# The down product of the last feed-forward, from float32 to three float32r products, in a four-layer gated cross-attention kernel

## The reference, cut to what matters

```
logits = x_flat @ router_w.T
probs = jax.nn.softmax(logits, axis=-1)
top_v, top_i = jax.lax.top_k(probs, K)            # K = 2, E = 8
top_v = top_v / jnp.sum(top_v, axis=-1, keepdims=True)
...
h = jax.nn.gelu(jnp.einsum('ech,ehf->ecf', expert_in, w1), approximate=False)   # h 256 -> f 1024
y = jnp.einsum('ecf,efh->ech', h, w2)                                            # f 1024 -> h 256
...
out = out + tok * (gate * keep.astype(x.dtype))[:, None]
```

## Time and profile before

| what | value |
|---|---|
| median of 3 runs | 1944.79 us (1943.92 to 1948.82) |
| the profiled execution's own time | 1942.3 us |
| its span in the trace | 1940.6 us |
| busy in the span: PE, PEld, DVE, ACT, POOL | 82%, 62%, 57%, 42%, 15% |
| the last feed-forward's tiles | from about 1643 us to the end |

### The profile page before, as it was taken

One profiled execution on the slowest core, in us unless ns is written; L12 is line 12 of the kernel. 1 busy time (PEld: TensorE's weight loads), 2 busy tenths in 40 slices (PEclk: granted clock), 3 DMA queues, 4 the chain that ended last, 5 costly groups with the idle time before them and its releaser, 6 DMA issues.

```text
span 1940.6 us, 29271 instructions
## 1 busy us (share of the span) xinstructions
PE 1598.8 (82%) x10374; PEld 1211.8 (62%) x10375; DVE 1104.1 (57%) x2555; ACT 817.6 (42%) x1817; POOL 300.2 (15%) x367
## 2 busy tenths in 40 slices
PE   5899883893888873578887999999969973999997
PEld 3566662782555542445554678788845552999997
DVE  5666628314899998766653454536459966222221
ACT  2455530323776742245554522213259951222221
POOL 2101100541121100111110000000111202333332
PEclk7899975897799987689988999999979985999999
DMA  7355234226554411534525000000266716422221
GB/s 162 53 81 78 45 121 178 44 36 123 113 115 95 84 55 46 77 51 69 70 34 219 24 1 1 1 0 1 58 88 103 123 63 231 152 38 38 33 37 28
DMA packets 86262, 144.10 MB, mean 74 GB/s; under 512 B 14032, under 2 KB 69768, under 8 KB 82938
## 3 DMA queue, kind: packets, MB, share of 16 engines
q1 hardware_dynamic: 66121, 102.76, 22.7%
q0 software_dynamic: 20016, 39.71, 12.8%
HBM read 75.50 MB, written 27.66 MB: 53 GB/s over the span
## 4 chain that ended last, share of the span: by engine, by line
PE 57%; DVE 24%; issue 6%; DMA 6%; ACT 4%; SPq 1%; POOL 0%; POOLq 0%; DVEq 0%; ACTq 0%
PE ps L1390 12%; PE ps L1498 7%; PE ps L1509 7%; PE ps L1359 4%; DMA Qpack<-QP 3%; DVE probs L2261 3%; PE ps L1030 3%; PE ps L886 2%; PE ps L977 2%; PE ps L1271 2%; PE ps L968 2%; PE ps L1280 2%; DVE hpart L2242 2%; PE ps L916 2%; PE ps L866 2%
## 5 line engine op out<-in xcount | busy, mean ns | idle before, releaser
L348 POOL DMA_DIRECT2D Kpack<-KP x192 | 101.1, 534 | 960.5 <-PE ps L1390 385.0
L1636 ACT ACTIVATE pT<-ps 128x512 f32<-128x512 f32 x256 | 151.7, 606 | 193.6 <-PE ps L971 100.0
L968 PE MATMUL ps<-Qpack,Kpack 99*128 99x256 bf16 (+1 forms) x768 | 167.6, 285 | 19.2 <-DMA Qpack<-MR 7.2
L1498 PEld LDWEIGHTS ps<-xgT,XNT 128*128 128x128 f32 x1248 | 147.7, 195 | 1.9
L1498 PE MATMUL ps<-xgT,XNT 128*128 128x128 f32 x1248 | 147.8, 278 | 0.0
L937 PE MATMUL ps<-Kpack,Qpack 97*128 97x256 bf16 x512 | 107.4, 298 | 42.1 <-DMA Qpack<-QP 19.0
L1509 PE MATMUL ps<-w,mid 128*128 x624 | 141.0, 379 | 0.0
L1918 ACT ACTIVATE mid<-ps 128x512 f32<-128x512 f32 x78 | 42.3, 595 | 202.9 <-PE ps L1498 202.9
L2162 DVE CUSTOM_DVE_ANT_0 Vb<-ps,mask_bf 128x256 bf16<-128x256 f32 x256 | 95.2, 419 | 55.2 <-PE ps L937 54.9
L1641 ACT ACTIVATE pT<-ps,nmax 128x256 f32<-128x256 f32 x256 | 120.4, 531 | 13.9 <-DVE nmax L2174 13.5
L1509 PEld LDWEIGHTS ps<-w,mid 128*128 128x128 f32 x624 | 115.6, 190 | 14.1
(11 more groups left out here) (318 smaller groups left out, 3265.3 us busy)
## 6 DMA issues: line engine op xcount, KB each, us to landing
Kpack<-KP POOLq DMA_DIRECT2D x192, 128.0 KB, 5.0
Qpack<-QP SPq DMA_DIRECT2D x192, 128.0 KB, 6.9
w<-in_w SPq DMA_DIRECT2D x16, 1024.0 KB, 6.3
ctxT<-in_ctxT SPq DMA_DIRECT2D x32, 256.0 KB, 7.8
h_rows<-in_h SPq DMA_DIRECT2D x16, 512.0 KB, 7.3
h<-h_rows SPq DMA_DIRECT2D x2, 4096.0 KB, 22.0
wd<-in_wd SPq DMA_DIRECT2D x4, 1536.0 KB, 14.3
xn_rows<-xn SPq DMA_DIRECT2D x16, 256.0 KB, 2.5
```

What stands on the lines that cost most here:

```text
L348: eng.dma_start(Kpack[j][DH * k:DH * (k + 1)].rearrange("d (e f) t -> d e (f t)", f=HALF), KP[par][:, part]).then_inc(done, 16)
L968: mm = pe.matmul(A[h % ring][:, t], Kpack[par][0:rows, h, t * P:(t + 1) * P], Qpack[par][0:rows, h], start=True, stop=L != 0)
L1498: mm = pe.matmul(bank[:, f % 4 * P:(f % 4 + 1) * P], w1_tile[k % 2][:, c, f * P:(f + 1) * P], xgT3[k % 2][:, c], start=c == 0, stop=c == K ...
L1636: act.activation(pT[h % 8][:], A[h % 2][:], ACT.Exp).then_inc(s["exp_done"], 1)
```

## The change

In `ffn3` alone, the down product is no longer made in float32. Both operands are written as a high part, rounded to float32r, and a low part, the rest, and for each of the 8 pieces PE makes three float32r products: high by high, high by low, low by high. For this:

- ACT, in `hidden`, makes the Gelu of each half twice, once to `mid3` in float32 and once to `mh3` in float32r (four instructions of 128 x 512 in place of two). DVE subtracts, `mid3` - `mh3`, in place, to `ml3` (`low_mid`, one instruction of 128 x 1024).
- The expert's w2 is split for each tile: ACT copies it in four pieces of 128 x 512 to `w2h_3` in float32r (`high_w2`), DVE subtracts each piece to `w2l_3` (`low_w2`). Both first read the expert's number into a register, which PE no longer does. `w2h_3` and `w2l_3` are single; they lie where X was. A piece may be overwritten when the down product of the tile before has used it (`f3_piece`, four counts a tile).
- The orders become, on ACT: hidden(t), high_w2(t), copy_w1(t+2); on DVE: copy_w1(t+2), low_mid(t), weigh(t-1), low_w2(t), copy(t+2). PE's order stays; down waits once for `ml3` and four times for a piece of `w2l_3`.
- Some semaphores of the two expert layers are merged under one name, with the counts shifted by a constant. ACT waits once, before its first Gelu, until X has been sent to DRAM; POOL waits for the same before its first gather.

```diff
@@ sbuf
-        X = sb("X", [P, NT, D], F32)
+        x_ctx = ExitStack()
+        X = sb("X", [P, NT, D], F32, x_ctx)
+        x_ctx.close()
+        X_r = sb("X_r", [P, NT, D], F32R)
...
-        mid3 = [sb(f"mid3_{i}", [P, HT, P], F32, f3c) for i in range(2)]
+        m3c = ExitStack()
+        mid3 = [sb(f"mid3_{i}", [P, HT, P], F32, m3c) for i in range(2)]
+        m3c.close()
+        ml3 = [sb(f"ml3_{i}", [P, HT, P], F32R, f3c) for i in range(2)]
         yg3 = [sb(f"yg3_{i}", [P, D], F32, f3c) for i in range(2)]
+        mh3 = [sb(f"mh3_{i}", [P, HT, P], F32R, f3c) for i in range(2)]
+        w2h_3, w2l_3 = (X_r[:, 8 * i:8 * i + 8] for i in range(2))
@@ tensor
                 def down(b, k):
                     t = GBUF * b + k
-                    e = expert(t)
-                    pe.wait_ge(s["f3_loaded"], e + 1)
-                    pe.wait_ge(s["f3_mid"], t + 1)
+                    pe.wait_ge(s["f3_ml"], t + 1)
                     wait(pe, s["f3_yg"], t - 1)
                     for c in range(HT):
-                        mm = pe.matmul(ps[5 + 2 * (k % 2)][:, 0], mid3[k % 2][:, c], w2_3[:, ds(e, 1), c].squeeze(1), start=c == 0, stop=c == HT - 1)
-                    mm.then_inc(s["f3_down"], 1)
+                        if c % 2 == 0:
+                            pe.wait_ge(s["f3_w2l"], W2_PIECES * t + c // 2 + 1)
+                        for j, (m, w) in enumerate(((mh3, w2h_3), (mh3, w2l_3), (ml3, w2h_3))):
+                            mm = pe.matmul(ps[5 + 2 * (k % 2)][:, 0], m[k % 2][:, c], w[:, c], start=c + j == 0, stop=c == HT - 1 and j == 2)
+                        if c % 2 == 1:
+                            mm.then_inc(s["f3_piece"], 1)
@@ scalar
                 def hidden(t, k):
                     act.wait_ge(s["f3_up"], t + 1)
-                    wait(act, s["f3_down"], t - 1)
+                    wait(act, s["f3_piece"], W2_PIECES * (t - 1))
                     for half in range(2):
-                        e = act.activation(mid3[k][:, 4 * half:4 * half + 4], UP3[k][half][:].rearrange("p a (c t) -> p (a c) t", t=P), ACT.Gelu)
+                        up = UP3[k][half][:].rearrange("p a (c t) -> p (a c) t", t=P)
+                        act.activation(mid3[k][:, 4 * half:4 * half + 4], up, ACT.Gelu)
+                        e = act.activation(mh3[k][:, 4 * half:4 * half + 4], up, ACT.Gelu)
                     e.then_inc(s["f3_mid"], 1)
+
+                def high_w2(t):
+                    e = act.value_load(expert3_i[0:1, ds(t, 1)], min_val=0, max_val=E3 - 1)
+                    act.wait_ge(s["f3_loaded"], e + 1)
+                    for p in range(W2_PIECES):
+                        wait(act, s["f3_piece"], W2_PIECES * (t - 1) + p + 1 if not isinstance(t, int) or t else 0)
+                        act.activation(w2h_3[:, 2 * p:2 * p + 2], w2_3[:, ds(e, 1), 2 * p:2 * p + 2].squeeze(1), ACT.Copy).then_inc(s["f3_w2h"], 1)
@@ vector
                 def weigh(t, k):
-                    dve.wait_ge(s["f3_down"], t + 1)
+                    dve.wait_ge(s["f3_piece"], W2_PIECES * (t + 1))
...
+                def low_mid(t, k):
+                    dve.wait_ge(s["f3_mid"], t + 1)
+                    dve.tensor_tensor(ml3[k][:], mid3[k][:], mh3[k][:], ALU.subtract).then_inc(s["f3_ml"], 1)
+
+                def low_w2(t):
+                    e = dve.value_load(expert3_i[0:1, ds(t, 1)], min_val=0, max_val=E3 - 1)
+                    for p in range(W2_PIECES):
+                        dve.wait_ge(s["f3_w2h"], W2_PIECES * t + p + 1)
+                        dve.tensor_tensor(w2l_3[:, 2 * p:2 * p + 2], w2_3[:, ds(e, 1), 2 * p:2 * p + 2].squeeze(1), w2h_3[:, 2 * p:2 * p + 2],
+                                          ALU.subtract).then_inc(s["f3_w2l"], 1)
+
                 def tile(t, k):
-                    if not isinstance(t, int) or t + 2 < RUN3:
+                    more = not isinstance(t, int) or t + 2 < RUN3
+                    if more:
                         copy_w1(t + 2, k)
+                    low_mid(t, k)
+                    if not isinstance(t, int) or t:
+                        weigh(t - 1, 1 - k)
+                    low_w2(t)
+                    if more:
                         copy(t + 2, k)
-                    weigh(t, k)
```

More of the change, by code:

```diff
@@ L77 @@
 PAIRS = NT // ST
+W2_PIECES = 4
 FREE = 1
@@ L316, in program @@
                  "experts_w0 experts_w1 experts_w2 experts_w3 experts_w4 experts_w5 experts_w6 experts_w7 "
-                 "f0_router f0_step f0_hot f0_list f0_idstep f0_idx "
+                 "router f0_step hot list f0_idstep f0_idx "
                  "f0_xt f0_xgT f0_up f0_mid f0_down f0_yg f0_scatter "
@@ L429, in low @@
             return x.bitcast(U16).rearrange("p (n two) -> p n two", two=2)[:, :, 0]
+        listed = E0 * (("ffn", 0) in stages)
         gathered = 16 * SL0 * (E0 // GBUF) * (("ffn", 0) in stages)
@@ L582, in ffn @@
                 if L == 0:
-                    sp.dma_start(wr0[:], a["wr0"]).then_inc(s["f0_router"], 16)
-                    sp.dma_start(br0[:], a["br0"].partition_broadcast(P)).then_inc(s["f0_router"], 16)
-                    sp.dma_start(bu0[:], a["bu0"]).then_inc(s["f0_router"], 16)
+                    sp.dma_start(wr0[:], a["wr0"]).then_inc(s["router"], 16)
+                    sp.dma_start(br0[:], a["br0"].partition_broadcast(P)).then_inc(s["router"], 16)
+                    sp.dma_start(bu0[:], a["bu0"]).then_inc(s["router"], 16)
                     send_rows(n, B - 1)
@@ L605, in ffn @@
                 else:
-                    sp.dma_start(wr3[:], a["wr3"]).then_inc(s["f3_router"], 16)
+                    sp.dma_start(wr3[:], a["wr3"]).then_inc(s["router"], 16)
                     for b in range(B - 2, B):
@@ L843, in layernorm @@
                     if pair == 1:
-                        pe.wait_ge(s[f"f{L}_router"], 48 if L == 0 else 16)
+                        pe.wait_ge(s["router"], 48 if L == 0 else 16 + 48 * (("ffn", 0) in stages))
                     if pair > 1:
@@ L1249, in lists @@
                 def lists(e):
-                    pe.wait_ge(s["f0_hot"], e + 1)
+                    pe.wait_ge(s["hot"], e + 1)
                     for t in range(NT):
@@ L1254, in lists @@
                                        lists0[:, e, t].rearrange("p v h -> p (v h)"), start=t == 0, stop=t == NT - 1)
-                    mm.then_inc(s["f0_list"], 1)
+                    mm.then_inc(s["list"], 1)
                 def turn(e):
@@ L1468, in ffn3 @@
                 for j in range(PAIRS3):
-                    pe.wait_ge(s["f3_hot"], j + 1)
+                    pe.wait_ge(s["hot"], listed + j + 1)
                     for t in range(NT):
@@ L1473, in ffn3 @@
                                        start=j + t == 0, stop=j == PAIRS3 - 1 and t == NT - 1)
-                mm.then_inc(s["f3_list"], 1)
+                mm.then_inc(s["list"], 1)
                 pe.wait_ge(s["f3_idx"], 1)
-                def expert(t):
-                    return pe.value_load(expert3_i[0:1, ds(t, 1)], min_val=0, max_val=E3 - 1)
                 def turn(b, k):
@@ L1928, in ffn3 @@
                         hidden(2 * i + k, k)
+                        high_w2(2 * i + k)
                         copy_w1(2 * i + k + 2, k)
@@ L1931, in ffn3 @@
                     hidden(t, t % 2)
+                    high_w2(t)
                     if t + 2 < RUN3:
@@ L2454, in softmax_rows @@
                 if L == 0:
-                    dve.wait_ge(s["f0_router"], 48)
+                    dve.wait_ge(s["router"], 48)
                     link(5 * r + 1, r, dve.tensor_tensor(route[2][:], logits, bc_exp(br0[:]), ALU.add))
@@ L2565, in hot @@
                     dve.tensor_tensor(hot0[e % 2][:], place0[:, :, e].unsqueeze(2).to_broadcast([P, NT, P]),
-                                      col[:].unsqueeze(1).to_broadcast([P, NT, P]), ALU.is_equal).then_inc(s["f0_hot"], 1)
+                                      col[:].unsqueeze(1).to_broadcast([P, NT, P]), ALU.is_equal).then_inc(s["hot"], 1)
                 def index(e):
-                    dve.wait_ge(s["f0_list"], e + 1)
+                    dve.wait_ge(s["list"], e + 1)
                     got = ps[3 + e % 2][:, 0, 0:5 * SL0].rearrange("p (v h) -> p v h", v=5)
@@ L2804, in route3 @@
                 chain(dve.tensor_scalar(expert3_i[:], expert3[:], E3 - 1.0, None, ALU.min))
-                dve.wait_ge(s["f3_list"], 1)
+                dve.wait_ge(s["list"], listed + 1)
                 got = ps[3][:].rearrange("p a b -> p (a b)")[:, 0:6 * TILES3].rearrange("p (v i) -> p v i", v=6)
@@ L2853, in ffn3 @@
                     tile(t, t % 2)
+                weigh(RUN3 - 1, (RUN3 - 1) % 2)
             for n, (kind, L) in enumerate(stages):
```

8 lines of the change are left out of this document (5 added, 3 removed).

## The result

| | before | after |
|---|---|---|
| median us (lowest to highest), 4 runs each | 1945.56 (1943.92 to 1948.82) | 1927.09 (1925.28 to 1929.23) |
| profiled execution, its span | 1942.3, 1940.6 | 1928.7, 1927.0 |

The ratio is 0.991, with a 95% interval of 0.9884 to 0.9936: 18.5 us faster by the medians, where 22 were forecast. The profile has only 13.6 us less. So there are two questions: whether the tiles got what the prediction gave them, and where some 4 to 8 us went.

What follows compares the result with a forecast made beforehand. PE was taken to bound the steady tiles at 7.25 us each; downs 1 to 36 save 0.61 us each, 22 in all, from the median 1944.8 to a forecast of 1923 us, own range 1917 to 1930.

Steps and rivals of the forecast that it cites:

- PE's part: Down on PE: 24 float32r products at 0.119 us, 2.85 in place of 3.46 us; period 7.25 to 6.64 us.
- The weight loads: Rival on PE: 24 weight loads at 0.190 us set the pace, 4.56 us a down, 42 us slower, 1987; chance 0.02.
- ACT's part: ACT's Gelus, four w2 copies (2.66 us) and w1 copy end at U + 5.82, 0.8 us less than the period.
- DVE's part: DVE's work with the new subtractions is 5.71 us a tile plus register-load gaps; it fits with little to spare.
- The first rival's case: Another engine sets the pace: DVE with both register gaps open, 7.07 us, 1938; or ACT at 7.2, 1943; chance 0.18.
- a sign of being wrong: The prediction is wrong if a register load keeps its gap behind queued work, or an ACT copy costs over 0.87 us.
- POOL: POOL's scatter and gather, held up to 0.7 us each by DVE's subtractions, total 4.3 of 6.64 us; nothing taken.
- Start: At the first tile, down(0) moves from ending at 1658.5 to starting at 1658.3 us's older schedule: gains 0.2 us.
- End: At the last tiles, down(38) waits for its subtractions; nothing gained or lost, the two end downs give nothing.
- The sum: Downs 1 to 36 save 0.61 us each, 22.0; the first 0.2, the rest nothing; forecast 1923 us.
- The range: Whole kernel: own range 1917 (product at 0.112 us) to 1930 (0.2 us a tile lost to waits).

Runs made afterwards that it cites:

- float32 run: Changed kernel, but PE makes down as 8 float32 products of the high parts, the low parts made but unused: 1946.39 us, period 7.25 us.
- run with one product: Changed kernel, but of PE's three down products only high by high is made, 8 in place of 24: 1882.78 us.
- both: Changed kernel with POOL's gather of tile t + 4 before scatter t and ACT's wait for X before its first w1 copies: 1921.70 us, ratio 0.9884.
- before, load at the gate: Kernel before the change, with the load of the last expert's weights held until the first tile's gate was applied: 1935.92 us.
- changed, again: The changed kernel without edits, run and profiled a second time: 1924.75 us, ratio 0.9903.
- last load just ahead: Changed kernel, with the load of the last expert's weights held until the first tile's gate was applied: 1927.94 us.
- table early: Changed kernel, with ACT's wait for X in DRAM before its first w1 copies, not before its first Gelu: 1924.67 us.

## Why the prediction was right, point by point

- **PE's part: right.** 24 x 0.119 = 2.85 us was forecast, 2.86 measured; a gain of 0.61 us a tile, 0.60 measured; a period of 6.64, 6.65 measured. The pace of the same form in another stage could be carried over. The float32 run shows that nothing else took part in it.
- **The weight loads: the rival is wrong.** PEld is busy for all of the 212.69 us, and the pace is 0.119. The Trainium skill's rule (Perfetto Trace Analysis, Identifying the Most-Contended Engine) takes this busy share, beside the share of peak FLOP/s, for the measure of headroom; here it left 6% before the change, and half as many loads again went with less time.
- **ACT's part: mis-sized, on the safe side.** Forecast was a wait of 0.8 us for up in each tile, it is 1.6. The term is 4 x 0.665 for the w2 copies: they last 0.65 each but start 0.52 apart, 2.21 us in all. That is 0.45 of the difference of 0.8; most of the rest is the same overlap between the Gelus, the copies and the w1 copy.
- **DVE's part: right in kind, mis-sized.** Four subtractions take 2.5 us and not 2.76, for the same reason (0.60 apart). The second register load leaves 0.42 us, forecast 0.25. That DVE "fits with little to spare" was too dark: the run with one product shows 1.1 us to spare. The first rival's case, a cycle near PE's with gaps of 0.7 us on both loads, does not occur: they are 0.58 and 0.42 us in the changed kernel. But the prediction's reason against it, that loads are covered when DVE is late, holds only in part. In the run with one product one load in two kept a gap of 0.5 to 1.0 us. This was named as a sign of being wrong; it did no harm because PE's period is 1.1 us longer.
- **POOL: the step that failed.** "the rows are gathered four tiles ahead, so I take nothing." The step weighed POOL's busy time, but not that its gather stands behind a scatter that waits for a gate which the change moves one step later, nor that the early gathers run while 2 MB loads are under way. It cost 3.67 us in the profiled execution, 1.5 of them by the clock that fell behind the gap, 1.9 in the second, and none in the runs in which the load came later. The hold by DVE's subtractions that the step did weigh, up to 0.7 us, did not come: the scatter takes 1.60 us. (The instruction that held the gather of the earlier trace rows is not the one shown beside it, which began while the gather was already held, but the one before, from 336.68 to 338.97 us.)
- **Start: a term left out.** Down(0) was to gain 0.2 us and lost 1.3. The table load, 1.28 us, stands in none of its terms: a second wait in front of the first Gelu put it on the path. With ACT's wait moved up ("both") down(0) ends 3.63 us behind the first up products, 0.04 sooner than before.
- **End: right.** From the start of the last up product to the end it is 21.3 us before (1940.6 less 1919.3) and 21.2 after (1927.0 less 1905.8).
- **The sum.** 22 forecast. In the profile 36 x 0.598 = 21.5, less 3.67 at tile 4, less 1.3 at down(0), less 0.6 ahead of the first up product (the product that begins the stage ran at a granted clock of 0.62, before at 0.69), and 1.4 more by the clock of the first up products: 17.3, and the stages differ by 17.4. In the second profile, whose clock is that of the kernel before, 21.5 less 1.9 less 1.3 are 18.3, and the stages differ by 18.4. The medians differ by 18.5.
- **The range.** 1927.1 lies in it by its upper end, which was set for 0.2 us a tile lost to waits. Nothing was lost so; what took its place were two losses that the prediction did not have. The tiles were right by their mechanism, the closeness of the rest was in part luck.

## What to carry to other kernels

When PE sets the pace, take the pace of the new product form from a stage that has it, and then lay the other engines' new work out in time over one period. Take instructions of one kind at the distance of their starts. Then follow what a moved instruction releases on a queue that the change does not touch: here a gate one step later held a scatter, and the gather behind it on POOL. A prefetch should not stand behind a wait for a result. It is the first tiles, while large loads still run, in which this shows. And where a product behind a gap is long, look at the granted clock before looking for a wait.

## What the runs showed of the hardware

- A gather of 128 KB that was issued 0.3, 0.5 and 1.9 us behind a 2 MB load landed after 7.5, 8.2 and 7.9 us (the last by the transposes' start); the median was 2.8 us. Issued 0.5 us ahead of the load in the kernel before it landed after 5.5 us, 0.8 ahead ("before, load at the gate") after 4.9, and neither was late.
- Behind a gap of 1.94 us in PE's work (changed, profiled) and one of 2.35 (one product) the granted clock fell to the lower level for 3.4 us. It stayed at 1.00 behind gaps of 1.65, 1.31 and 0.80 us ("changed, again", "last load just ahead", "float32 down"). The gap alone does not tell: with one product the clock also fell at 1659.0 us, behind a gap of 1.66 and a down(0) that kept waiting for its pieces.
- POOL's scatter took 1.62 us on average before and 1.60 after the change, but 2.27 us in the run with one product. What decides is what runs when it starts. Between 1680 and 1860 us of the changed kernel 26 of 27 scatters start just ahead of DVE's subtractions and last 1.6 us, though these run beside them for 1.6 us; the one that starts under a subtraction takes 2.05. With one product all 33 start under one and last 1.6 to 3.6 us. The Trainium skill (SBUF — State Buffer, Who interferes with whom) says that a VectorE instruction with two SBUF inputs contends with a GpSimd instruction that reads SBUF, and that the order of issue decides which of them waits; the trace agrees. DVE's subtraction did not get longer (0.68 us there, 0.69 with pauses).
- The table load, 1.28 us, ran ahead of the wait of the first Gelu where this had only the wait for up (before, and "table early"), and behind it, on the path, where a second wait stood in front. That the second wait itself does it, and not its place behind the w1 copies, is read from these runs, not tried apart.
- The first 5 us of the stage's up products ran at a mean granted clock of 0.82 in one execution and of 0.52 in another of the same kernel; the first period was 13.1 and 14.5 us by it.
